# A two-layer selective-scan block on one core: projections read in pixel order, one copy moved a unit on, and the start of layer 1 rearranged

## The reference, cut to what matters

```python
# layer 0: 8 directions k; xs[k] is u (channels x 1024 pixels) in the direction's order,
# a snake over rows, mirrored rows or columns, forward or backward
x_dbl = einsum('bkdl,kcd->bkcl', xs, x_proj_weight[k])     # 12 + 16 + 16 rows
delta = softplus(dt_projs_weight[k] @ dts + bias)          # 384 x 1024
for l in range(1024):                                      # for each of 16 states n
    h[n] = exp(delta*A[n]) * h[n] + delta*u * B[n];  y += h[n] * C[n]

# layer 1: 4 directions (rows and columns, forward and backward), one set of weights
dt = softplus((u @ W_x)[:12] @ W_dt + b_dt)
decay = exp(cumsum(dt*A[n])); h = decay * cumsum(dt*u*B[n] / (decay + 1e-12)); y += h * C[n]
```

## Time and profile before

| | |
|---|---|
| median of three runs | 17118.56 us |
| profiled execution, its own time | 17104.75 us |
| its span, first to last instruction | 17103.0 us |
| busy: VectorE | 15041.9 us (88%) |
| busy: GpSimd | 13820.5 us (81%) |
| busy: TensorE matmul | 13081.6 us (76%) |
| busy: ScalarE | 8696.2 us (51%) |
| mean granted TensorE clock | 0.912 of full speed |

### The profile page before, as it was taken

One profiled execution on the slowest core, in us unless ns is written; L12 is line 12 of the kernel. 1 busy time (PEld: TensorE's weight loads), 2 busy tenths in 40 slices (PEclk: granted clock), 3 DMA queues, 4 the chain that ended last, 5 costly groups with the idle time before them and its releaser, 6 DMA issues.

```text
span 17103.0 us, 102091 instructions
## 1 busy us (share of the span) xinstructions
PE 13081.6 (76%) x29328; PEld 5263.8 (31%) x29328; DVE 15041.9 (88%) x9070; ACT 8696.2 (51%) x7907; POOL 13820.5 (81%) x5869
## 2 busy tenths in 40 slices
PE   7777777777777787777877778777777777777777
PEld 2322333323333233322333323332233332333323
DVE  8998889988899888998889988899888998889988
ACT  4445744457444574445744456444574445644456
POOL 7987779877798777987779877798777987779877
PEclk9998989989899998999989989899898998989989
DMA  5552245522455224552255522555225552255522
GB/s 171 194 182 93 74 169 195 181 95 74 172 194 180 94 74 170 195 182 93 74 172 194 182 94 73 172 193 182 93 73 176 192 182 92 73 175 191 182 91 73
DMA packets 688754, 2442.01 MB, mean 143 GB/s; under 512 B 78396, under 2 KB 100168, under 8 KB 688200
## 3 DMA queue, kind: packets, MB, share of 16 engines
q1 hardware_dynamic: 688200, 2435.49, 41.1%
HBM read 2419.45 MB, written 15.73 MB: 142 GB/s over the span
## 4 chain that ended last, share of the span: by engine, by line
PE 31%; DVE 25%; POOL 18%; issue 17%; DMA 5%; ACT 3%; DVEq 0%; SPq 0%; POOLq 0%; ACTq 0%
PE bank L465 14%; POOL room L778 13%; DVE room L936 8%; DVE room L928 8%; DMA room<-bc_rows 5%; DVE room L998 4%; PE bank L474 4%; PE bank L419 4%; PE bank L341 3%; DVE room L1018 3%; POOL room L787 3%; PE bank L499 2%; PE bank L396 2%; PE bank L385 2%; POOL room L753 1%
## 5 line engine op out<-in xcount | busy, mean ns | idle before, releaser
L928 DVE TENSOR_TENSOR_SCAN room<-bank,room 128x1024 f32<-128x1024 f32 x3072 | 6954.7, 2278 | 551.8 <-ACT bank L594 551.5
L778 POOL TENSOR_TENSOR room<-room 128x1024 f32<-128x1024 f32 x3072 | 7167.1, 2365 | 262.6 <-DMA room<-bc_rows 208.6
L419 PE MATMUL bank<-room,identity 128*128 128x512 f32 x12288 | 6266.9, 638 | 499.1 <-DVE room L936 324.1
L594 ACT ACTIVATE bank<-room,a 128x1024 f32<-128x1024 f32 x3072 | 3412.4, 1116 | 4295.4 <-DVE room L928 4282.5
L465 PE MATMUL bank<-room,identity 128*128 128x512 f32 x6144 | 3128.1, 657 | 1046.4 <-DVE room L1018 895.8
L998 DVE TENSOR_TENSOR_SCAN room<-bank,room 128x1024 f32<-128x1024 f32 x1536 | 3438.5, 2274 | 59.4 <-POOL room L825 45.1
L419 PEld LDWEIGHTS bank<-room,identity 128*128 128x128 f32 x12288 | 2439.8, 203 | 3204.0 <-issue 2304.2
L936 DVE TENSOR_TENSOR room<-room,bank 128x1024 f32<-128x1024 f32 x2360 | 2822.2, 1196 | 284.3 <-PE bank L406 279.2
L406 PE MATMUL bank<-parts,pick_row 96*128 96x512 bf16 x4720 | 1488.8, 398 | 1695.7 <-DVE room L936 1638.3
L825 POOL TENSOR_TENSOR room<-room 128x1024 f32<-128x1024 f32 x768 | 2301.3, 3019 | 30.1
L787 POOL TENSOR_TENSOR room<-room 128x1024 f32<-128x1024 f32 x712 | 1678.4, 2357 | 740.0 <-DVE room L928 740.0
(11 more groups left out here) (88 smaller groups left out, 9344.4 us busy)
## 6 DMA issues: line engine op xcount, KB each, us to landing
room<-bc_rows SPq DMA_DIRECT2D x4552, 512.0 KB, 4.4
wx<-in_w_x SPq DMA_DIRECT2D x65, 162.0 KB
bc_rows<-xdbl SPq DMA_DIRECT2D x72, 128.0 KB, 4.2
xT<-in_x SPq DMA_DIRECT2D x8, 768.0 KB, 5.7
out_x<-xT SPq DMA_DIRECT2D x8, 768.0 KB, 4.3
win<-in_w_in SPq DMA_DIRECT2D x16, 288.0 KB, 3.2
room<-in_w_in SPq DMA_DIRECT2D x16, 288.0 KB, 5.4
room<-in_w_out SPq DMA_DIRECT2D x16, 288.0 KB, 5.8
```

The source lines that it names most:

```text
L419: ins = nc.tensor.matmul(bank[:, YACC + h, :], identity[:, :], state0[:, g % STATES, halves(h)], start=(n == 0), stop=(n == N - 1))
L594: nc.scalar.activation(whole(DECAY0[g % 2]), delta0[:, j, :], ACT.Exp, scale=a0[:, col:col + 1]).then_inc(S["decay"], note("decay", (i, j, ...
L778: nc.gpsimd.tensor_tensor(source0[:, g % SOURCES, :], du0[:, j, :], b_ring0[:, g % BROWS, :], ALU.mult).then_inc(S["source"], note("source ...
L928: nc.vector.tensor_tensor_scan(run(state0[:, g % STATES, :]), run(whole(DECAY0[g % 2])), run(source0[:, g % SOURCES, :]), 0.0, ALU.mult, A ...
```

## The change

In layer 0, `take_dt` comes after the decay of the next unit (n = 7 in place of 6). `x_proj` reads u as it lies, 512 columns at a time; the half that it makes is in pixel order, and `take_xd` puts it in scan order with two copies of 256 columns, whose source in PSUM is reversed, or for the column directions strided by 32. The raw steps of a direction now wait for both halves.

In layer 1, the running sums of group 0 take their factor from an element of PSUM (written by a memset). The three raw steps lie in the bank pairs WORK, DECAY_ROWS and YACC, which leaves HSUM free for that element. GpSimd makes du of group 0 ahead of the units, and du of group j + 1 after unit n = 12 of group j. The softplus of group 2 moves from ahead of the units to behind the decays of unit 1.

```diff
--- before.py
+++ after.py
@@ -187,7 +187,7 @@
                  "xz", "silu", "mm", "ev", "stat", "gs", "xn", "pad", "conv", "u",
                  "p1", "r1", "p2", "parts", "parts_pool", "dl", "du",
                  "decay", "source", "scan", "spread", "weigh", "weigh_pool", "sum",
-                 "dcol", "cs", "drows", "dcols", "gate", "source1", "gated", "gated_last", "scan1", "hsum", "weigh1", "sum1",
+                 "dcol", "cs", "drows", "dcols", "gate", "source1", "gated", "gated_last", "ones", "scan1", "hsum", "weigh1", "sum1",
                  "yinit", "yev", "cen", "sq", "rs", "nrm", "aff", "gat", "res"]
         S = {n: semaphore("s_" + n) for n in names}
         note, at = counts.note, counts.at
@@ -372,19 +372,10 @@
                 if i == 0:
                     pe.wait_ge(S["u"], at("u", (l, J - 2), b))
                     pe.wait_ge(S["ev"], at("ev", ("conv", l, 1), b))
-                if l == 1:
-                    work(b, h, ("xd", 1, 0, h), [], [(wx1[:, j, :], u[:, j, halves(h)]) for j in range(J)], rows=XR + R)
-                    return
-                pe.wait_ge(S[f"load_wx{i % 2}"], at(f"load_wx{i % 2}", i, b))
-                eighth = SIDE // 4
-                wait_free(b, h)
-                dst = stored(bank[0:XR + R, WORK[h], :])
-                for line in range(2):
-                    for j in range(J):
-                        rhs = lines(u[:, j, :], SCANS[i][1])[line][:, h * eighth:(h + 1) * eighth, :]
-                        ins = nc.tensor.matmul(dst[line], wx[:, i % 2, j, :], rhs, start=(j == 0), stop=(j == J - 1))
-                ins.then_inc(S["mm"], note("mm", ("xd", 0, i, h)))
-                free[h] = ("ev", ("xd", 0, i, h))
+                if l == 0:
+                    pe.wait_ge(S[f"load_wx{i % 2}"], at(f"load_wx{i % 2}", i, b))
+                w = [wx[:, i % 2, j, :] if l == 0 else wx1[:, j, :] for j in range(J)]
+                work(b, h, ("xd", l, i, h), [], [(w[j], u[:, j, halves(h)]) for j in range(J)], rows=XR + R)
 
             def dt_proj(b, l, i, j, banks=WORK):
                 w = wdt[XR:XR + R, i % 2, :] if l == 0 else wdt1[XR:XR + R, :]
@@ -392,7 +383,7 @@
                     wait_free(b, 0, 1)
                     free[0] = free[1] = ("ev", ("dt", l, i, j))
                 for h in range(2):
-                    pe.wait_ge(S["ev"], at("ev", ("xd", l, i, h), b))
+                    pe.wait_ge(S["ev"], at("ev", ("xd", l, i, h if l else 1), b))
                     ins = nc.tensor.matmul(bank[:, banks[h], :], w[:, j * P:(j + 1) * P], xdbl[XR:XR + R, halves(h)],
                                            start=True, stop=True)
                 ins.then_inc(S["mm"], note("mm", ("dt", l, i, j)))
@@ -447,7 +438,7 @@
             def scans1(b):
                 for h in range(2):
                     x_proj(b, 1, 0, h)
-                for j, banks in enumerate((WORK, (YACC, YACC + 1), (HSUM, HSUM + 1))):
+                for j, banks in enumerate((WORK, (DECAY_ROWS, DECAY_ROWS + 1), (YACC, YACC + 1))):
                     dt_proj(b, 1, 0, j, banks)
 
                 def add_direction(m, q):
@@ -468,6 +459,8 @@
                 def add_weighted(m):
                     j, n = UNITS1[m]
                     pe.wait_ge(S["weigh1"], at("weigh1", (j, n), b))
+                    if m == 0:
+                        pe.wait_ge(S["dl"], at("dl", (1, 0, J - 1), b))
                     if n == 0 and j > 0:
                         pe.wait_ge(S["yev"], at("yev", (1, j - 1), b))
                     for h in range(2):
@@ -554,7 +547,21 @@
                     nc.scalar.activation(u[:, j, :], u[:, j, :], ACT.Silu).then_inc(S["u"], note("u", (l, j)))
 
             def take_xd(b, l, i, h):
-                take(b, ("xd", l, i, h), xdbl[:, halves(h)], h, rows=XR + R)
+                if l == 1:
+                    take(b, ("xd", l, i, h), xdbl[:, halves(h)], h, rows=XR + R)
+                    return
+
+                order, half = SCANS[i][1], SIDE // 2
+                act.wait_ge(S["mm"], at("mm", ("xd", 0, i, h), b))
+                for line in range(2):
+                    if order == "cols":
+                        k = h if line == 0 else 1 - h
+                        part = (slice(None), slice(None), slice(k * half, (k + 1) * half))
+                    else:
+                        part = (slice(None), slice(h * half // 2, (h + 1) * half // 2), slice(None))
+                    ins = nc.scalar.activation(stored(xdbl[:, :])[line][part],
+                                               lines(whole(WORK[0])[0:XR + R], order)[line][part], ACT.Copy)
+                ins.then_inc(S["ev"], note("ev", ("xd", 0, i, h)))
 
             def first_part(b, i):
                 act.wait_ge(S["ev"], at("ev", ("xd", 0, i, 1), b))
@@ -614,8 +621,7 @@
                             first_part(b, p[1])
                     elif p and p[0] == "z":
                         take(b, ("z", 0, p[2], p[3]), gate[0][:, p[2], halves(p[3])], p[3])
-                    p = piece(g - 1)
-                    if p and p[0] == "dt":
+                    elif p:
                         take_dt(b, p[1], p[2])
 
                     ahead = i * J + j + 1
@@ -677,10 +683,10 @@
 
                 softplus1(b, 0, WORK[0])
                 columns(0)
-                softplus1(b, 1, YACC)
-                softplus1(b, 2, HSUM)
+                softplus1(b, 1, DECAY_ROWS)
                 act.wait_ge(S["dcol"], at("dcol", 0, b))
                 decay_cols(0)
+                act.wait_ge(S["dl"], at("dl", (1, 0, 1), b))
                 decay_rows(0)
                 gates(0, 0, 1, 2)
                 gates(1, 0, 1, 2)
@@ -691,6 +697,8 @@
                     if m + 1 < len(UNITS1):
                         decay_cols(m + 1)
                         decay_rows(m + 1)
+                    if m == 0:
+                        softplus1(b, 2, YACC)
                     if m + 2 < len(UNITS1):
                         gates(m + 2, 2)
                     if n == 2 and j + 1 < J:
@@ -804,8 +812,7 @@
                         third_part(b, i + 1)
 
             def scans1(b):
-                for j in range(J):
-                    du(b, 1, 0, j)
+                du(b, 1, 0, 0)
                 for m, (j, n) in enumerate(UNITS1):
                     if n == 0:
                         pool.wait_ge(S["du"], at("du", (1, 0, j), b))
@@ -827,6 +834,8 @@
                         else:
                             nc.gpsimd.tensor_tensor(state, state, src, ALU.mult).then_inc(
                                 S["gated"], note("gated", (j, n, q)))
+                    if n == 12 and j + 1 < J:
+                        du(b, 1, 0, j + 1)
 
             def make_taps(l):
                 nc.gpsimd.tensor_tensor(
@@ -964,7 +973,9 @@
                 collect(b, PASSES - 1)
 
             def scans1(b):
+                nc.vector.memset(bank[:, HSUM, 0:1], 1.0).then_inc(S["ones"], note("ones", 0))
                 init_y(b, 1)
+                dve.wait_ge(S["ones"], at("ones", 0, b))
 
                 def sum_of_steps(j, q):
                     if q == SUMS1[0] and j >= 2:
@@ -978,7 +989,9 @@
                     dst = csum[j % 2][:, q, :]
                     if q % 2:
                         src, dst = src[:, ::-1], dst[:, ::-1]
-                    nc.vector.tensor_tensor_scan(dst, one[:, :].broadcast_to([P, T]), src, 0.0,
+
+                    ones = bank[:, HSUM, 0:1] if j == 0 else one[:, :]
+                    nc.vector.tensor_tensor_scan(dst, ones.broadcast_to([P, T]), src, 0.0,
                                                  ALU.mult, ALU.add).then_inc(S["cs"], note("cs", (j, q)))
 
                 def scan1(m, q):
```

## The result

The changed kernel takes 16596.33 us, the median of four runs (16575.25 to 16607.99), against 17112.8 for the kernel before (four runs, 17105.59 to 17120.23). The ratio is 0.9697, 95% interval 0.968 to 0.9714: 3.0% faster, 19 us from the predicted 16615. The profiled execution took 16589.09, its span 16587.3, at a mean granted clock of 0.926 (before 0.912).

A forecast was written before the change was run, and what follows sets the result against it. VectorE's scans and weighs, busy 88% of the span, were taken as the bound, their waits as what can be won. 270 + 166 - 2 + 68 = 502 us off gave 16615 us, range 16450 to 16750.

The forecast's parts named there:

- Part 1: Layer 0, raw steps' copy one unit later: scan 7 stops waiting for ScalarE's decay; 270 us, range 170 to 420.
- T + 4.5: New start of the weigh of n = 6 at full clock, T being the end of the weigh of n = 4; before, T + 7.58.
- 8.5 and 9.64: Weigh starts at n = 6, in us after the weigh of n = 4, at low clock; TensorE's chain sets them, no gain.
- 209 and 485: Bounds in us for moving the raw steps' copy: TensorE's chain at today's clocks, or all 176 events at full clock.
- the lateness: How far weighs of n = 6 start behind 4.38 us after the weigh of n = 4 ends; 572 us over 176 events before.
- I took 10 us off: Group 0, source 9: GpSimd waits for a late B row behind SyncE's queue; first direction only, 219 becomes 209 us.
- Part 2: Layer 0 x projection read contiguously: column directions win 2.59 us each, 64 times, 166 us; ordering hidden; range 110 to 180.
- Part 3: Start of layer 1: VectorE's first scan at 1501.3 in place of 1509.86, 8.5 us an image, 68 us; range 40 to 80.
- the first rival: TensorE keeps it all: low clock falls as often on the n = 6 events; copy move gives 209 us, time 16700; 20%.
- The clock recovered: Rival: with TensorE idle less, all raw-step events run at full clock; copy move gives 485 us, time 16402; 12%.
- GpSimd became a bound: Rival: sources at n = 12 to 15 late by 1.5 us in groups 0 and 2; 144 us go back, 16760; 10%.
- The clock didn't fall more often: Denies the rival that low stretches of TensorE's clock increase, with 300 more the time is 17247, slower; 3%.

The follow-up runs named there:

- p1_copy_later: Kernel before with only the copy of the raw steps (take_dt) moved behind the decay of n = 7: 16849.5 us, ratio 0.9847.
- a_weights_later: Changed kernel with the next x projection's weights' load and SyncE's wait before it moved from group 0, n = 8 to group 1, n = 0: 16558.4 us.
- a_no_order: Changed kernel with one plain copy of 512 columns for every x projection, the ordering left out: 16591.4 us, ratio 0.9694.
- a_sum_behind: Changed kernel with TensorE's sum of state n = 4 (7, 10) put behind the next C row: 16620.8 us, ratio 0.971.

## Why the prediction was right

*Part 1* was forecast at 270 us and came in at 265 alone. The step that carried it, T + 4.5 at full clock, was exact; so was the one that TensorE's chain is untouched at the low clock (8.5 and 9.64 before and after). The choice between 209 and 485 was a judgement, and that it came out within 5 us is in part luck: alone the lateness fell by 280 us and 16 us were lost outside layer 0, and in the changed kernel it fell by 308. On GpSimd I took 10 us off, for the first direction alone. Scans 9 and 12 wait 25 us in the changed kernel (in p1_copy_later 23), in the first direction and in later ones, because more group 0 events now run at full clock (21 of 64 for the 5 us behind T, before 8), where source 9 ends behind the wanted scan. But TensorE's late rows would have held most of that time anyway: these waits cost 9 us in the changed kernel and 3 in p1_copy_later. So the 10 was about right, and not for the reason given. That the cause of these waits is SyncE's queue was right, and a_weights_later shows it.

*Part 2*, 166 us: the waits behind column projections fell by 185 us in the changed kernel and 169 alone. The 16 between them are no gain of this part: GpSimd's late source 9 holds VectorE there and hides the wait, as their return in a_weights_later shows (52.6 us). The ordering copy was charged too much: 0.76 us for two, not 0.77 to 1.25, since the stride costs nothing; it was hidden either way (a_no_order). The Trainium skill (Advanced Engine Details and Errata, Memory Cachelines) has an access to SBUF that changes the 16-byte line each time at a penalty; the trace agrees, contiguous reads halved TensorE's time. For a strided read of PSUM by ScalarE no cost was seen (381 ns either way).

*Part 3*, 8.5 us an image: 8.3. The chain of the softplus, the tables, the decays and the gate was right to 0.2 us. What was not said is how little of it needs du inside the units: with the ones in PSUM, a second du ahead costs nothing. Between the layers only 50 us were won in the changed kernel, not 66, because in seven images the first layer's tail has one more stretch of low clock (3.4 us, 16 us behind the last scan) and is 2.2 us longer, before anything of this part begins.

*The sum*, 502, against 516 in the medians and in the spans. Stage by stage it is 434 against 453 in layer 0 and 68 against 63 behind it. The closeness is better than the method: the parts alone measured 265, 123 and 80, and part 2 fell short by 43 us where the clock was low in worse places. A sum of parts can't be trusted here to better than some 50 us.

*The rivals*: TensorE did keep what it had in each event at the low clock (the first rival's mechanism), but in fewer of them. The clock recovered in part. GpSimd became a bound only at n = 9 and 12 of group 0, where it cost 9 us and not 144. The clock didn't fall more often in all (410 low stretches for 444), though in a_sum_behind it did (509), and that kernel is slower than the changed one.

*What would show it*: ScalarE's wait 10 us (said under 40); TensorE's 338 (said 294 to 394, of it 94 behind the projections, where it is 68); records of 592 ns; 12.1 us; sums of 2.27. The rest as said.

## What to carry to other kernels

A wait that names one engine may only be the first of two: sort the events by when the engine behind it would be ready, and price the removal by the second. The same holds for what a repair is worth: 23 us of waits for late B rows went, and 21 came back under TensorE's name. An in-order queue makes a copy's place matter more than its length: a decay that was ready 3 us earlier stood behind it, and moving one line was worth 1.5%. Reordering work on the engine that is late in itself moves the wait and doesn't remove it.

## What the runs showed of the hardware

- TensorE reads a moving operand strided by 128 bytes (float32) at half the pace: 12 records of 256 columns in 5.41 us, contiguous 2.8. The record's duration (608 against 379 ns) understates it.
- ScalarE reads PSUM with a stride of 32 float32 words as fast as contiguously: 381 ns for 256 columns by rows and by columns; from SBUF the same stride costs 1997 to 2013 ns for 1024 columns against 1030.
- A scan on VectorE with both inputs in SBUF and a GpSimd product run one after the other (4.36 and 4.33 us each); with a one-element factor in PSUM, broadcast, both have their full rate (2.27 and 2.36).
- The same is seen in layer 1's units of the changed kernel, where the sums of groups 1 and 2 still have their factor in SBUF: a sum takes 2.4 us, and the GpSimd product that starts beside it ends 2 us late, 4.33 or 4.73 us for 2.35 or 2.87.
- Idle work for TensorE made a kernel faster: 1.3 us of constant matmuls in idle stretches of 3 us, mean granted clock 0.926 to 0.932, 39 us.
